# Token index tables of the experts: one row of 32 products instead of four groups of eight

## What is computed

```python
xn = layernorm(x)
attn = linear_attention(xn)            # 16 heads of 32, relu features weighted with cos and sin of the position
probs = softmax(einsum('bsd,ed->bse', xn, choice_w))      # E = 8 experts
G, I = top_k(swapaxes(probs, -1, -2), 1024)               # each expert chooses 1024 tokens of each batch entry
x_in = take_along_axis(xn[:, None], I[..., None], axis=2)
h = silu(einsum('bekd,edf->bekf', x_in, w1))              # 512 -> 1024
x_mlp = einsum('bekf,efd->bekd', h, w2)                   # 1024 -> 512
out = x + attn @ W_out + b_out + scatter_add(G[..., None] * x_mlp at I)
```

## Time and profile before

| | |
|---|---|
| median of 3 runs | 2501.93 us (2501.14 to 2505.41) |
| profiled execution, own time | 2501.82 us |
| its span | 2500.0 us |
| mean granted TensorE clock | 0.984 |
| TensorE busy | 2398.0 us, 96% |
| VectorE busy | 1342.9 us, 54% |
| GpSimd busy | 1078.0 us, 43% |
| ScalarE busy | 831.2 us, 33% |
| list products (L1382) | 512, 169 ns each by the record |
| marks (L907, `one_lo`) | 64, 1218 ns each |

### The profile page before, as it was taken

The page is one execution under the profiler, slowest core; times in us unless marked ns, Lnnn a source line. Parts: engine busy times, 40 slices in busy tenths (PEclk is TensorE's granted clock), DMA queues, the critical chain, the costliest instruction groups (busy, mean ns, idle before and its releaser), DMA issues.

```text
span 2500.0 us, 34669 instructions
## 1 busy us (share of the span) xinstructions
PE 2398.0 (96%) x12544; PEld 2012.5 (80%) x12544; DVE 1342.9 (54%) x2654; ACT 831.2 (33%) x1458; POOL 1078.0 (43%) x959
## 2 busy tenths in 40 slices
PE   8999999999999999999999999998998999999898
PEld 7889988898999887777777787787787787787677
DVE  7777777687787795434335245245245344335331
ACT  4545544445454552222213213223223222223111
POOL 0100034200002565664565565565566566466541
PEclk9999999999999999999999999999999999999999
DMA  7555434455544455224224224323323323332222
GB/s 197 160 134 135 109 54 74 69 136 151 134 118 83 60 89 123 49 41 111 48 46 107 50 48 94 56 51 78 76 49 75 77 51 77 72 50 47 37 39 30
DMA packets 125947, 205.38 MB, mean 82 GB/s; under 512 B 28264, under 2 KB 53480, under 8 KB 125552
## 3 DMA queue, kind: packets, MB, share of 16 engines
q0 software_dynamic: 57088, 118.02, 26.5%
q1 hardware_dynamic: 68720, 85.42, 11.6%
HBM read 119.22 MB, written 100.93 MB: 88 GB/s over the span
## 4 chain that ended last, share of the span: by engine, by line
PE 84%; issue 6%; DVE 5%; another core or an unknown queue 2%; DMA 1%; ACT 1%; POOL 0%; POOLq 0%; DVEq 0%; SPq 0%; ACTq 0%
PE ps L1355 27%; PE ps L1357 26%; PE ps L1356 26%; PE ps L1448 2%; DVE h_lo L1322 1%; PE ps L1585 1%; DVE h_hi L1320 1%; DMA xo<-in_L_attn_x_dram 1%; PE ps L1382 1%; DMA normed_rows<-xo 0%; DVE one_lo L907 0%; ACT hf L773 0%; DVE stats L811 0%; DVE w_lo L1326 0%
## 5 line engine op out<-in xcount | busy, mean ns | idle before, releaser
L461 POOL DMA_INDIRECT rows<-normed_rows,idx_row x512 | 539.0, 1053 | 156.5 <-issue 156.5
L1355 PE MATMUL ps<-w_hi,h_hi 128*128 128x512 f32 x1024 | 412.7, 403 | 42.2 <-DVE h_lo L1322 21.0
L571 POOL DMA_INDIRECT out_dram<-y,idx x128 | 227.1, 1774 | 482.1 <-ACT y L793 480.0
L1355 PE MATMUL ps<-xi_hi,w_hi 128*128 128x512 f32 x1024 | 407.4, 398 | 8.5 <-issue 8.3
L1356 PE MATMUL ps<-w_lo,h_hi 128*128 128x512 f32 x1024 | 406.6, 397 | 5.8 <-issue 5.7
L1357 PE MATMUL ps<-w_hi,h_lo 128*128 128x512 f32 x1024 | 406.2, 397 | 4.6 <-issue 4.4
L1320 DVE CAST h_hi<-hf 128x512 fp32r<-128x512 f32 x256 | 111.3, 435 | 556.6 <-issue 292.2
L1356 PE MATMUL ps<-xi_lo,w_hi 128*128 128x512 f32 x1024 | 403.0, 394 | 1.6 <-issue 1.6
L1357 PE MATMUL ps<-xi_hi,w_lo 128*128 128x512 f32 x1024 | 401.5, 392 | 0.0
L773 ACT ACTIVATE hf<-ps 128x512 f32<-128x512 f32 x256 | 153.0, 598 | 678.5 <-PE ps L1357 437.6
L1355 PEld LDWEIGHTS ps<-w_hi,h_hi 128*128 128x128 f32 x1024 | 196.9, 192 | 96.8 <-issue 30.4
(11 more groups left out here) (176 smaller groups left out, 4117.3 us busy)
## 6 DMA issues: line engine op xcount, KB each, us to landing
xo<-in_L_attn_x_dram SPq DMA_DIRECT2D x32, 512.0 KB, 4.6
normed_rows<-xo SPq DMA_DIRECT2D x32, 512.0 KB, 4.9
out_dram<-bo POOLq DMA_DIRECT2D x16, 1024.0 KB, 9.1
out_dram<-xo POOLq DMA_DIRECT2D x64, 256.0 KB, 3.9
w_raw<-in_L_ffn_w_dram SPq DMA_DIRECT2D x32, 512.0 KB
w_raw<-in_L_ffn_w_dram SPq DMA_DIRECT2D x8, 2048.0 KB, 9.4
xn<-normed_rows SPq DMA_DIRECT2D x96, 128.0 KB, 2.5
rows<-normed_rows,idx_row POOLq DMA_INDIRECT x512
```

The costliest lines, as they stand in the source:

```text
L461: nc.gpsimd.indirect_dma_start(rows[:, tt, a, :], None, pieces[:, :], bass.IndirectOffsetOnAxis(ap=idx_row[:, b, tile, a:a + 1], axis=0)). ...
L571: nc.gpsimd.indirect_dma_start(of[:, :], bass.IndirectOffsetOnAxis(ap=idx[:, u * TPB + tt:u * TPB + tt + 1], axis=0), y[:, tt, :], None, c ...
L1355: nc.tensor.matmul(dst, a_hi, b_hi, start=start, stop=False, skip_group_check=True)
```

## The change

`one_lo` gets four buffers of eight tiles, the wait ahead of the third and fourth part goes, and all 32 products stand in one row behind the last up tile, m = 7, with one wait for all four parts. `list_pe` is raised by four at the end of the row, so that it counts on as before. The first list is not touched.

```diff
-            one_lo = sb("one_lo", [P, 2, 8, P], BF16)
+            one_lo = sb("one_lo", [P, 4, 8, P], BF16)
...
             def list_part(e, b, turn, c, into):
 
-                if turn > 0 and c >= 2:
-                    dve.wait_ge(list_pe, AHEAD + turn * 4 + c - 1)
...
                             elif 2 <= m <= 5:
-                                list_part(of_e, of_b, turn, m - 2, one_lo[:, m % 2, :, :])
+                                list_part(of_e, of_b, turn, m - 2, one_lo[:, m - 2, :, :])
...
-            def make_list(turn, c):
-
-
-                if c == 0:
-                    pe.wait_ge(fin, AHEAD + B * NT)
-                    pe.wait_ge(idx_ready, AHEAD + turn)
-                pe.wait_ge(list_dve, turn * 4 + (c + 1))
-                for j in range(8):
-                    last = nc.tensor.matmul(ps[:, 4, 16:32], one_lo[:, c % 2, j, :], pay[:, c * 8 + j, :],
-                                            start=(c == 0 and j == 0), stop=(c == 3 and j == 7),
-                                            skip_group_check=True)
-                last.then_inc(list_pe, 1)
+            def make_list(turn):
+
+                pe.wait_ge(fin, AHEAD + B * NT)
+                pe.wait_ge(idx_ready, AHEAD + turn)
+                pe.wait_ge(list_dve, turn * 4 + 4)
+                for j in range(NT):
+                    last = nc.tensor.matmul(ps[:, 4, 16:32], one_lo[:, j // 8, j % 8, :], pay[:, j, :],
+                                            start=j == 0, stop=j == NT - 1, skip_group_check=True)
+                last.then_inc(list_pe, 4)
...
-                        if u % HALVES == 0 and m >= 4:
-                            make_list(e * B + (u // HALVES + 1), m - 4)
+                        if u % HALVES == 0 and m == KF - 1:
+                            make_list(e * B + (u // HALVES + 1))
```

## The result

The changed kernel took **2521.84 us** (median of 22 runs, 2501.99 to 2537.64); the kernel before, on the same chip beside it, 2505.43 us (22 runs, 2492.59 to 2519.92). The ratio is **1.0074, 95% interval 1.0055 to 1.0093**: slower by 0.7%, where 2495.8 us and a gain were forecast, and outside the range of 2483 to 2512. The profiled execution took 2528.25 us (span 2526.4), 26.4 us more span than the one before.

A forecast was written before the change was run, and what follows sets the result against it. The prediction took TensorE, busy 96% of the span, to bound the kernel. Gains of 4.0 us (dense lists) and 2.0 us (disturbed lists) took 2501.8 us to 2495.8 us, range 2483 to 2512.

The forecast's parts named there:

- Part 1: Eight dense lists: the row costs 0.97 us instead of 1.48, gaining 0.5 us per list, 4.0 us in all.
- Part 2: Eight disturbed lists: instructions reach TensorE at a limited rate; three fewer per list gain 0.25 us each, 2.0 us.
- slower rival: Seven first units: row of 32 starves, 11 us, until the gathers end; 2.8 us lost each, 2517 us; chance 0.2.
- instructions gathering ahead of the row in a halt: Argument against the slower rival: a halt ahead of the row lets instructions gather, as before expert 3's fourth group.
- Part 3: VectorE's third and fourth marks lose their waits on groups of products: two waits per list go, worth nothing.
- cover of the two waits: VectorE's second halt, 3.69 us in expert 3; if it shrinks, up to 1.8 us come free in such a unit.
- Part 4: VectorE's end of the list waits for 32 products instead of 8: no cost, unless the room goes.
- room: In the dense unit, VectorE reaches the list's end 2.0 us after the row's results are there.
- R2: Much faster rival: the wait for ScalarE ahead of m = 7 goes, 1.9 us in seven units; 2485 us, chance 0.2.
- limit until the gathers end: Disturbed first units: a limit on how fast instructions reach TensorE until GpSimd's 20 gathers end, 0.17 us per instruction.

The follow-up runs named there:

- set B: Second set of follow-up runs, each ratio taken within the set, on another occasion; the kernel before took 2375.9 us in it.
- set E: Fifth set of follow-up runs, with the gains' gathers moved apart too; the kernel before took 2374.87 us in it.
- set C: Third set of follow-up runs, repeating earlier variants and the changed kernel; the kernel before took 2602.74 us in it.
- four_buffers: The kernel before with four mark buffers and without VectorE's two waits, groups of eight kept: 2520.74 us, ratio 1.0054.
- set A: First set of follow-up runs, asking what in the change costs the time; the kernel before took 2504.74 us in it.
- waits_kept_again: The kernel before with four mark buffers, VectorE's two waits kept: 2605.59 us, ratio 1.0007, in set C; as waits_kept, 2375.73 us, 0.9999, in set B.
- row_held: The changed kernel with VectorE held ahead of the third and fourth marks: 2366.6 us, ratio 0.9960, in set B; 2640.23 us, 1.0149, in set C.
- gains_between_after: The changed kernel with pauses between its gathers and one gain gather ahead of each scatter of y: 2368.68 us, ratio 0.9975 to the kernel before.
- set D: Fourth set of follow-up runs, with the train of gathers shortened or broken by pauses; the kernel before took 2616.52 us in it.
- paced_after: The changed kernel with all gathers kept but waits between them: 2377.05 us, ratio 0.9093 to the kernel before.
- row_later: The changed kernel with the row behind the second down tile and the spread behind the third: 2503.51 us, ratio 1.0005 to the kernel before.

## Why the prediction was wrong

**Part 1 was right as a price.** The row takes 0.82 us wherever the stream is dense, and a list gains 0.53 us against the 0.5 forecast. Where all 16 lists are dense that is 8.5 us, and sets B and E measured 9.3 and 8.4.

**Part 2 is the step that failed**: "their order matters little: the same number gets through by the same moment", and the 2.0 us gained from it. The stretch was read as a bound on the supply of instructions, with their number as the price. The trace of after and set C show two things together: instructions arrive by ones and twos, as read, but TensorE's signals to the other engines also arrive up to 10 us late, and both from 10 us or more into the train of 20 gathers until some 3 us behind its end. I take it that with groups of eight a halt falls partly on waits that are there anyway, while the row puts 32 tiny products, which cover nothing, where the stream is thinnest, and all of the down projection behind them. It took 9.4 us (the slower rival had said 11), and half-clock products followed; the seven first units lost 18.2 us where that rival's price was 19.6.

The slower rival's mechanism and place were right. That its numbers came so near is in part luck: the 2.8 us a unit were the middle of 0.3 to 5.4, experts 2 to 6 lost 3.2 to 4.5 each, expert 7 lost 1.8 and expert 1 gained 2.0, and the 2517 us had a gain of 4.0 in the third units in them, which lost 9.7. What spoke against it, instructions gathering ahead of the row in a halt, didn't help: in expert 3's unit TensorE halted for 1.00 us ahead of m = 7 (its first product starts at 1543.04), and 14 products ran through; in the other starved rows of that trace it was 13 to 24.

The depth of 64 that the Trainium skill gives TensorE's queue ("TensorE: Matmul & The Clock Gate", section "Architectural detail: the array is 16× 32×32, not 1× 128×128") would be 32 products with their weight loads; 14 ran through, and no row shows the depth or how full the queue was. The Trainium skill ("TensorE: Matmul & The Clock Gate", section "HAM oscillation — how this bites in real kernels") says that what follows a gap in the stream runs cold. The trace agrees, but this is the smaller part: the nine products behind the row, 0.43 us apart, took 3.9 us instead of 2.0, while the row took 8.6 us too long.

**Part 3** named the cover of the two waits and then priced them at nothing. four_buffers took them alone and lost 16 us in set A. waits_kept_again clears the buffers' place, on another occasion. But holding VectorE again saved nothing in set C (1.0149 against 1.0150), so with the row in place the waits don't set the time. four_buffers itself was run in set A only, and why VectorE running ahead hurts with groups of eight stays open.

**Part 4** failed by its own condition, "unless that room goes". The 2.0 us of room were against an on-time signal; the row's signal came 6.9 us late, and the third units lost 9.7 us where 7 x 0.5 was to be gained. In set C this is the larger loss of the two. That four groups, with a signal each, spare these units on the same occasions (28.67 us in four_buffers) is measured; how they do it is not.

Under all of it lies that one trace was taken for the kernel. Half the lists had a price of the occasion in them, and R2's "coupling" and the "limit until the gathers end" were two sides of one cause that the change doesn't touch. **The change gains 0.3 to 0.4% where signals are on time and costs 0.7% to 1.5% where they aren't.** The first half is read from two variants of it (row_held in set B, gains_between_after in set E); the changed kernel itself never ran on a quiet occasion. With the gathers spread it gained 8.4 us in set E and 2.9 in set D, the latter hardly clear of noise, and the pacing itself is worth 9% of the time on the one disturbed occasion on which it was tried: paced_after at 2377 us stands against 2617 for before and 2653 for the changed kernel in the same set.

**Open:** what makes an occasion disturbed, the chip or the moment, why it is TensorE's signals alone that come late, and where the backlog sits. No run here varies it.

## What to carry to other kernels

When halts end together with a train of GpSimd's gathers, try a pause inside the train before anything is moved on the engines that halt: here one of 2.5 to 3.3 us in each train, with shorter ones in some, took 237 us off on a disturbed occasion, where the largest gain from anything done on TensorE, on a milder one, was 22. A wait that "costs nothing" in one trace may be what keeps a stream together, and tiny products in a row have nothing to hide a late supply behind, so a row wants a place where the stream is dense; behind the second down tile (row_later, set A) it lost nothing, but gained nothing either. Take the kernel before again in every set, and mistrust a price that was read in a disturbed stretch of a single trace.

## What the runs showed of the hardware

- TensorE's signals to other engines are recorded within 0.01 us of its products' ends on one occasion and up to some 10 us late on another, for the same kernel (waits_kept and waits_kept_again), with GpSimd's own spans (0.94 to 1.24 us a gather in the unit shown) and the gathers' transfers unchanged. The signals of VectorE, ScalarE and GpSimd are within 0.01 us on both.
- It needs a train of gathers: in the unit shown the first sign came 13 us into it, in others of that trace from 10 us on, and it is over some 3 us behind the train's end. 8 gathers left signals up to 1.6 us late, and 8 and 12 with 3 us between up to 3.3 us, with nearly all units dense.
- Halts of TensorE then cost twice, since the products behind them ran 0.43 us apart instead of 0.23 for some 4 us and more.
- The occasion made 240 us of 2375, some thirty times the worth of the change.
